# Routed experts by sorted blocks in place of dense expert units

## Chip, cores and metric

The kernel runs on 1 core of one Trainium2 chip. The metric is the device time of one execution in microseconds, the median of several runs.

## What is computed

Two transformer layers over x of 2 x 512 tokens with 256 features: a grouped-query attention with ternary weights, a gated MLP of width 1024 with a Walsh-Hadamard transform, a time-mixing recurrence (scan over the tokens) and a mixture of experts. Each part is normalised, goes through its layer, is normalised again and added to x. The change lies in the last part, here cut to its core:

```python
logits = x @ gate_w                      # E = 32 experts
probs = jax.nn.softmax(logits, axis=-1)
topw, topi = jax.lax.top_k(probs, K)     # K = 4
topw = topw / jnp.sum(topw, axis=-1, keepdims=True)
combine = jnp.zeros((T, E), x.dtype).at[jnp.arange(T)[:, None], topi].set(topw)
def body(acc, ew):
    wg_e, wu_e, wd_e, c_e = ew           # F = 96 features per expert
    h = jax.nn.silu(x @ wg_e) * (x @ wu_e)
    return (acc + c_e[:, None] * (h @ wd_e), None)
out, _ = jax.lax.scan(body, jnp.zeros_like(x), (wg, wu, wd, combine.T))
shared = jax.nn.silu(x @ sg) * (x @ su) @ sd     # SF = 704 features
out = out + jax.nn.sigmoid(x @ seg) * shared
```

## The kernel before

The program is written by hand, one instruction stream an engine, with semaphores between them (`wait_ge`, `then_inc`). Tokens are kept as 8 tiles of 128 rows (`xa`, `xb`); a batch b is four of them, T = 512 tokens. For products the rows are transposed to columns and split into two fp32r parts, high and low (`cols_hi`, `cols_lo`), and each product is three passes (hi x hi, lo x hi, hi x lo; `three_passes`, L1472 to L1474).

The features of all experts and of the shared expert are laid in one row of E*F + SF = 3776 and cut into MC = 30 chunks of 128. Every chunk is computed for every token of a batch, so there are 60 expert units v. Of a unit, SP loads the chunk's weights (`load_chunk`, 384 KB, into one of four places), ACT casts them to the high part (`chunk_high`, L1298), POOL subtracts for the low part (`chunk_low`, L638). PE makes gate and linear product (`expert_up`: twelve matmuls of 512 columns), ACT takes the silu (L1240), DVE multiplies (`expert_unit`, L1095), and PE's select matmul (L1680) spreads each token's weight of the expert over the chunk's features:

```python
pe.matmul(ps[:, (3 * r + 2) % 4, :], select_sb[:, bass.ds(chunk * P, P)],
          ct[:, cs], start=True, stop=True).then_inc(bc_full, 1)
```

A token that didn't choose the expert has weight 0 there. DVE multiplies by it (L1100), ACT and DVE split the result (L1246, L1104), and PE adds it to the output (`expert_down`, twelve matmuls of 256 columns, L1484) in PSUM; the down product of unit v - 1 stands behind the up product of unit v.

The order of the work is written out. The 30 units of batch 0 are interleaved by hand with the time mixing of batch 1 (`keys`, `values`, `receptances` after units 2, 3 and 6, the output product after 14, batch 1's transposes and logits after 18 to 20; on DVE `mixes`, `read_keys`, `scan`, `out_stats`, `out_apply`, `in_apply`), so batch 1's mixing is spread over 20 units. Two units on, batch 1's 30 follow, most of them in a loop of four units. Routing (`route_top`, `route_weights`, `route_split`, L1012 to L1076) finds the four largest logits of each token. After the last unit DVE takes statistics of the output in PSUM (`out_stats`), POOL raises the variance to -1/2 (`power`, L518), DVE and ACT scale, add and shift (`out_apply`, `shift`) and SP stores.

## Time and profile before

| | us |
|---|---|
| runs shown: median (lowest to highest) | 691.62 (690.61 to 692.38) |
| span of the profiled execution, from its first to its last instruction | 690.5 |
| PE busy in it | 581.9 |
| DVE busy | 451.5 |
| ACT busy | 311.6 |
| POOL busy | 251.7 |
| batch 0's first unit starts | 370.7 |
| last matmul starts | 681.3 |

The profile's page gives no other time of that execution; its span stands within the runs shown. Busy times overlap: a matmul's record reaches from its start to its last write, and the next one starts before that, so the distance between two starts is what a matmul costs in a stream. Durations are of one execution, on the one core.

### The profile page before, as it was taken

To read this page: it belongs to the slowest core of one execution; us is meant where nothing else is said; L and a number is where in the kernel's file an instruction comes from. 1 tells how busy PE (TensorE), PEld (TensorE's weight loads), DVE (VectorE), ACT (ScalarE), POOL (GpSimd) and SP (SyncE) were. 2 spreads that over 40 slices of the span, in tenths; PEclk is the share of its full clock that TensorE was granted. 3 is DMA by queue.
4 is the path that set the end of the run, shared out by engine and by line. 5 is a ranking of instruction groups with operands and counts; after the bars stand their busy time and mean duration, and the time that the engine had idled before them with its cause. 6 is when DMAs were issued, how large, how long until landed. Compare 5 with 4: busy or idle time off the path is not lost.

```text
span 690.5 us, 11130 instructions
## 1 busy us (share of the span) xinstructions
PE 581.9 (84%) x3618; PEld 420.6 (61%) x3618; DVE 451.5 (65%) x881; ACT 311.6 (45%) x511; POOL 251.7 (36%) x294
## 2 busy tenths in 40 slices
PE   0358999999998897988626879998989989999994
PEld 0244544554443486766524667886768868888883
DVE  5898767877773667555888658758675464444444
ACT  1132556666676532275115563433534444444442
POOL 5821233343447314031030632443324434444440
PEclk9976599999999999999768989999999999999998
DMA  6063210111330013000020112231222222222310
GB/s 171 0 162 97 59 38 22 34 35 36 112 111 1 12 47 58 0 1 1 0 91 0 47 47 68 84 101 46 69 69 78 89 82 80 88 89 90 91 54 30
DMA packets 25627, 41.22 MB, mean 60 GB/s; under 512 B 3640, under 2 KB 17272, under 8 KB 25592
## 3 DMA queue, kind: packets, MB, share of 16 engines
q1 hardware_dynamic: 25160, 39.72, 19.5%
q0 software_dynamic: 432, 1.05, 0.9%
q8 instruction: 20, 0.33, 0.2%
q14 instruction: 15, 0.12, 0.1%
HBM read 37.81 MB, written 3.80 MB: 60 GB/s over the span
## 4 chain that ended last, share of the span: by engine, by line
PE 57%; DVE 25%; issue 7%; ACT 6%; POOL 3%; DMA 1%; SPq 1%; POOLq 0%; DVEq 0%; ACTq 0%
PE ps L1484 9%; PE ps L1472 7%; PE ps L1473 7%; PE ps L1474 7%; PE ps L1424 7%; PE ps L1553 6%; PE ps L1435 6%; PE ps L1427 2%; DVE st L756 2%; DVE xn L684 2%; ACT h_hi L1246 2%; DVE hf L1100 2%; DVE sg L1095 2%; PE ps L1680 1%; DVE negm L844 1%
## 5 line engine op out<-in xcount | busy, mean ns | idle before, releaser
L638 POOL TENSOR_TENSOR mslot_lo<-mraw,mslot_hi 128x768 fp32r<-128x768 f32 x60 | 112.2, 1870 | 176.7 <-ACT mslot_hi L1298 176.7
L844 DVE TENSOR_REDUCE negm<-ps 128x1 f32<-128x512 f32 (+2 forms) x192 | 107.6, 593 | 36.7 <-PE ps L1427 35.6
L1246 ACT CAST h_hi<-hf 128x512 fp32r<-128x512 f32 x76 | 47.2, 621 | 181.3 <-DVE hf L1100 144.1
L1208 ACT ACTIVATE probs<-ps 128x512 f32<-128x512 f32 x160 | 91.9, 597 | 66.7 <-PE ps L1435 66.0
L1472 PE MATMUL ps<-cols_hi,mslot_hi 128*128 128x512 f32 x240 | 96.4, 402 | 3.7 <-ACT sg L1240 2.2
L1473 PE MATMUL ps<-cols_hi,mslot_lo 128*128 128x512 f32 x240 | 94.3, 393 | 0.0
L1474 PE MATMUL ps<-cols_lo,mslot_hi 128*128 128x512 f32 x240 | 93.7, 390 | 0.0
L1095 DVE TENSOR_TENSOR sg<-sg,ps 128x512 f32<-128x512 f32 x60 | 41.0, 683 | 75.0 <-PE ps L1474 58.3
L1484 PE MATMUL ps<-mslot_hi,h_hi 128*128 128x256 f32 x240 | 78.0, 325 | 9.0 <-DVE h_lo L1104 9.0
L1424 PE MATMUL ps<-k_all,q_all 72*128 (+4 forms) x256 | 73.8, 330 | 9.2 <-DMA q_all<-q_parts_scratch 7.4
L1104 DVE TENSOR_TENSOR h_lo<-hf,h_hi 128x512 fp32r<-128x512 f32 x60 | 41.5, 692 | 41.2 <-ACT h_hi L1246 41.2
L1435 PE MATMUL ps<-q_all,k_all 75*128 (+4 forms) x256 | 65.9, 321 | 3.1 <-ACT probs L1208 2.3
L1484 PE MATMUL ps<-mslot_hi,h_lo 128*128 128x256 f32 x240 | 67.7, 282 | 0.0
L1484 PE MATMUL ps<-mslot_lo,h_hi 128*128 128x256 f32 x240 | 67.7, 282 | 0.0
L518 POOL TENSOR_TENSOR rstd<-ve,halfneg 128x4 f32<-128x4 f32 x16 | 16.2, 1011 | 119.3 <-DVE ve L787 72.7
L1240 ACT ACTIVATE sg<-ps 128x512 f32<-128x512 f32 x76 | 45.2, 595 | 27.2 <-PE ps L1474 26.0
L1424 PEld LDWEIGHTS ps<-k_all,q_all 72*128 72x128 bf16 (+1 forms) x256 | 25.9, 104 | 49.9 <-issue 30.1
L1427 PE MATMUL ps<-hide_cols,identb 128*128 128x128 bf16 x256 | 54.7, 234 | 0.0
L1472 PEld LDWEIGHTS ps<-cols_hi,mslot_hi 128*128 128x128 f32 x240 | 45.7, 190 | 14.3 <-ACT sg L1240 3.1
L1484 PEld LDWEIGHTS ps<-mslot_hi,h_hi 128*128 128x128 f32 x240 | 46.1, 192 | 11.5 <-DVE h_lo L1104 11.4
L1474 PEld LDWEIGHTS ps<-cols_lo,mslot_hi 128*128 128x128 f32 x240 | 45.2, 188 | 10.1
L1298 ACT CAST mslot_hi<-mraw 128x768 fp32r<-128x768 f32 x60 | 49.8, 831 | 2.3 <-PE ps L1484 2.3
(221 smaller groups left out, 1176.7 us busy)
## 6 DMA issues: line engine op xcount, KB each, us to landing
mraw<-in_moe_w SPq DMA_DIRECT2D x60, 384.0 KB, 3.1
q_all<-q_parts_scratch SPq DMA_DIRECT2D x48, 96.0 KB
q_parts_scratch<-qparts SPq DMA_DIRECT2D x6, 256.0 KB, 2.5
k_parts_scratch<-kparts SPq DMA_DIRECT2D x6, 192.0 KB, 3.8
k_all<-k_parts_scratch SPq DMA_DIRECT2D x6, 192.0 KB
xa<-in_x SPq DMA_DIRECT2D x2, 512.0 KB, 4.9
w2a<-in_w SPq DMA_DIRECT2D x1, 1024.0 KB, 8.0
w1raw<-in_w SPq DMA_DIRECT2D x2, 512.0 KB, 5.4
```

Of the source, the lines that this page charges most:

```text
L638: pool.tensor_tensor(mslot_lo[:, place, :], mraw[:, place, :], mslot_hi[:, place, :].bitcast(F32), ALU.subtract)\
L844: dve.tensor_reduce(negm[:, par, qt, h0:h0 + nh], ps[:, u % 4, 0:nh * w].rearrange("p (h t) -> p h t", h=nh), AX.X, ALU.max, negate=True). ...
L1095: dve.tensor_tensor(sg[:, par, :], sg[:, par, :], ps[:, (3 * r + 1) % 4, :], ALU.mult).then_inc(t_done, 1)
L1208: act.activation(probs[:, par, u, :], ps[:, 4 + u % 2, :], ACT.Exp)\
L1246: act.copy(h_hi[:, par, :], hf[:, par, :]).then_inc(h_hi_done, 1)
L1424: pe.matmul(ps[:, u % 4, c:c + w], q_all[0:72, bass.ds(g * (GQ * T) + (h * T + qt * P), P)], k_all[0:72, bass.ds(g * T, w)], start=True, s ...
L1427: mm = pe.matmul(ps[:, u % 4, c + w - P:c + w], identb[:, :], hide_cols[:, :], start=False, stop=True)
L1435: mm = pe.matmul(ps[:, 4 + u % 2, c:c + w], k_all[0:75, bass.ds(g * T + kt * P, P)], q_all[0:75, bass.ds(g * (GQ * T) + (h * T + kt * P), w)],
L1472: pe.matmul(out, lhs_hi, rhs_hi, start=first, stop=False)
L1473: pe.matmul(out, lhs_lo, rhs_hi, start=False, stop=False)
L1474: return pe.matmul(out, lhs_hi, rhs_lo, start=False, stop=last)
L1484: mm = pe.matmul(z_tile(part, b, t), h[:, par, ts], w, start=start and n == 0 and t % 2 == 0, stop=False, skip_group_check=True)
```

## The change

The routed experts are computed only for tokens that chose them. All of this is new: for each (token, choice) the row gets a place in a DRAM table `x_sorted` of 63 blocks of 128 rows, each block of one expert. 63 = 4096 / 128 + 31 bounds what any routing can need. PE counts, with triangular and all-one matrices, how many tokens ahead chose the same expert (`ranks`); DVE turns ranks into destinations and the blocks' experts into a table (`route_places`, `block_experts`), batch 0 first, so that batch 0's rows can go before batch 1's routing is known. ACT copies each row four times with its number n*4 + j behind it (`rows_with_ids`, 260 floats), and POOL scatters tile by tile with indirect DMAs (`scatter`, 32 in all). The table is filled with padding rows first, by seven DMAs of SP, whose number is out of bounds.

The shared expert keeps the old way, in six chunks of its own (`shared_up`, `shared_down`, 12 units u = 16 + s for both batches), without select matmul; ACT multiplies the result with the token's sigmoid gate (`shared_rows`). Batch 1's mixing now stands between the six units of batch 0; ranks and the table's row stand between those of batch 1. The weights of all experts are loaded once into SBUF (`wgu` 6.3 MB, `wd` 3.1 MB, fp32).

Then come 63 blocks. SP loads a block's rows, PE transposes them, reads the block's expert from `etab` into a register, multiplies with its gate and up weights (fp32, 2 x 96 columns), transposes the gated result and multiplies with its down weights; DVE copies the transposes out and gates, ACT does silu and the output copy, POOL scatters the 128 output rows to `y_slots` by their numbers, out-of-bound ones skipped. At the end SP loads `y_slots`, four rows a token, and DVE adds them with the token's weights (`combine`, L1348 of the changed file).

```diff
+FIRST_SHARED = E * F // P
+SHARED = MC - FIRST_SHARED
+BLOCKS = N * TOPK // P + E - 1
+XW = D + 4
+XR, YR, CR = 4, 4, 4
...
+            sp.wait_ge(s_pad, 2)
+            for n in range(7):
+                sp.dma_start(
+                    x_sorted[n * 9 * P:(n + 1) * 9 * P, :].rearrange("(b p) f -> p b f", p=P),
+                    pad[:, :].unsqueeze(1).to_broadcast((P, 9, XW))).then_inc(s_sorted, 16)
...
+            sp.wait_ge(proj_r, DC * B)
+            load_up(1)
+            sp.wait_ge(z_done, 2 * B)
+            load_up(0)
+
+            for r in range(2):
+                sp.wait_ge(scattered[r], 16 * TOPK * TILES // 2)
+            for i in range(BLOCKS):
+                if i >= XR:
+                    sp.wait_ge(bt_done, i - XR + 1)
+                    sp.wait_ge(bt_copied, i - XR + 1)
+                sp.dma_start(xblk[:, i % XR, :], x_sorted[i * P:(i + 1) * P, :])\
+                    .then_inc(xb_in[i % XR], 16)
+            for r in range(YR):
+                sp.wait_ge(y_out[r], 16 * len(range(r, BLOCKS, YR)))
+            for t in range(TILES):
+                if t >= CR:
+                    sp.wait_ge(yc_read, t - CR + 1)
+                sp.dma_start(
+                    ycomb[:, t % CR, :, :].rearrange("p j d -> p (j d)"),
+                    y_slots.rearrange("(t p j) d -> t p (j d)", p=P, j=TOPK)[t])\
+                    .then_inc(yc_in[t % CR], 16)
             for b in range(B):
...
+            def scatter(u):
+
+                pool.wait_ge(dest_ready, u // TPB + 1)
+                pool.wait_ge(xr_ready, 2 * u + 2)
+                for j in range(TOPK):
+                    pool.indirect_dma_start(
+                        out=x_sorted, out_offset=bass.IndirectOffsetOnAxis(
+                            ap=dest[:, u, j:j + 1], axis=0),
+                        in_=xr[:, u % 2, j, :], in_offset=None).then_inc(scattered[u % 2], 16)
...
+            for i in range(BLOCKS):
+                pool.wait_ge(by_ready, i + 1)
+                pool.indirect_dma_start(
+                    out=y_slots, out_offset=bass.IndirectOffsetOnAxis(
+                        ap=ids[:, i:i + 1], axis=0),
+                    in_=yblk[:, i % YR, :], in_offset=None, bounds_check=N * TOPK - 1,
+                    oob_is_err=False).then_inc(y_out[i % YR], 16)
...
+            def block_in(i):
+
+                dve.wait_ge(bt_done, i + 1)
+                if i >= 2:
+                    dve.wait_ge(bu_done, i - 1)
+                dve.tensor_copy(xcol[:, i % 2, :], ps[:, i % 2, 0:D])
+                dve.tensor_copy(ids[:, i:i + 1], xblk[:, i % XR, D:D + 1]).then_inc(bt_copied, 1)
...
+            def block_gate(i):
+
+                dve.wait_ge(b_silu, i + 1)
+                if i >= 2:
+                    dve.wait_ge(bh_done, i - 1)
+                dve.tensor_tensor(hb[:, i % 2, :], gb[:, i % 2, :], ps[:, 2 + i % 2, F:2 * F],
+                                  ALU.mult).then_inc(b_mul, 1)
...
+            def block_hidden(i):
+
+                dve.wait_ge(bh_done, i + 1)
+                if i >= 2:
+                    dve.wait_ge(bd_done, i - 1)
+                dve.tensor_copy(hcol[0:F, i % 2, :], ps[0:F, 6 + i % 2, 0:P])\
+                    .then_inc(bh_copied, 1)
...
+                            ins = dve.scalar_tensor_tensor(
+                                xa[:, t, :], ycomb[:, t % CR, j, :], wtop[:, t, j:j + 1],
+                                xa[:, t, :], ALU.mult, ALU.add)
...
+            def rows_with_ids(u):
+
+                act.wait_ge(rows_ready, (NORMS.index((2, u // TPB)) + 1) * TPB)
+                act.wait_ge(s_ids, 1)
+                if u < 2:
+                    act.wait_ge(m_lo_ready, SHARED)
+                else:
+                    act.wait_ge(scattered[u % 2], 16 * TOPK * (u // 2))
+                act.copy(xr[:, u % 2, :, 0:D],
+                         rows[:, u, :].unsqueeze(1).to_broadcast((P, TOPK, D))).then_inc(xr_ready, 1)
+                act.copy(xr[:, u % 2, :, D:XW],
+                         idf[:, u, :].unsqueeze(2).to_broadcast((P, TOPK, XW - D)))\
+                    .then_inc(xr_ready, 1)
...
+            def block_silu(i):
+
+                act.wait_ge(bu_done, i + 1)
+                if i >= 2:
+                    act.wait_ge(b_mul, i - 1)
+                act.activation(gb[:, i % 2, :], ps[:, 2 + i % 2, 0:F], ACT.Silu)\
+                    .then_inc(b_silu, 1)
...
+            def block_out(i):
+
+                act.wait_ge(bd_done, i + 1)
+                if i >= YR:
+                    act.wait_ge(y_out[i % YR], 16 * (i // YR))
+                act.copy(yblk[:, i % YR, :], ps[:, 4 + i % 2, 0:D]).then_inc(by_ready, 1)
...
+            def block_in(i):
+
+                pe.wait_ge(xb_in[i % XR], 16 * (i // XR + 1))
+                if i >= 2:
+                    pe.wait_ge(bt_copied, i - 1)
+                else:
+                    pe.wait_ge(silu_done, B * (HC + SHARED))
+                    pe.wait_ge(mul_done, B * (HC + SHARED))
+                for k in range(DC):
+                    mm = pe.transpose(ps[:, i % 2, k * P:(k + 1) * P],
+                                      xblk[:, i % XR, k * P:(k + 1) * P], ident[:, :])
...
+            def block_up(i, e):
+
+                pe.wait_ge(bt_copied, i + 1)
+                if i >= 2:
+                    pe.wait_ge(b_mul, i - 1)
+                for k in range(DC):
+                    mm = pe.matmul(
+                        ps[:, 2 + i % 2, 0:2 * F].rearrange("p (w f) -> p w f", w=2),
+                        xcol[:, i % 2, k * P:(k + 1) * P], wgu[:, k, :, bass.ds(e * F, F)],
+                        start=k == 0, stop=k == DC - 1)
+                mm.then_inc(bu_done, 1)
...
+            def block_hidden(i):
+
+                pe.wait_ge(b_mul, i + 1)
+                if i >= 2:
+                    pe.wait_ge(bh_copied, i - 1)
+                pe.transpose(ps[0:F, 6 + i % 2, 0:P], hb[:, i % 2, :], ident[:, :])\
+                    .then_inc(bh_done, 1)
...
+            def block_down(i, e):
+
+                pe.wait_ge(bh_copied, i + 1)
+                if i >= 2:
+                    pe.wait_ge(by_ready, i - 1)
+                pe.matmul(ps[:, 4 + i % 2, 0:D], hcol[0:F, i % 2, :],
+                          wd[0:F, bass.ds(e, 1), :].rearrange("p o d -> p (o d)"),
+                          start=True, stop=True).then_inc(bd_done, 1)
...
-            expert_up(0, 0, 0, 0)
-            for v in range(1, MC):
-                expert_up(v, v % 4, 0, v)
-                expert_down(v - 1, (v - 1) % 4, 0, start=v == 1)
...
-            with pe.Fori(0, (MC - 2) // 4) as i:
-                for r in range(4):
-                    q = (MC + 2 + r) % 4
-                    expert_up(i * 4 + (MC + 2 + r), q, 1, i * 4 + (2 + r))
-                    expert_down(i * 4 + (MC + 1 + r), (q + 3) % 4, 1)
-            expert_down(2 * MC - 1, (2 * MC - 1) % 4, 1)
...
+            shared_up(6)
+            ranks(1)
+            shared_up(7)
+            shared_down(6)
+            block_row()
+            for s in range(8, 2 * SHARED):
+                shared_up(s)
+                shared_down(s - 1)
+            shared_down(2 * SHARED - 1)
...
+            experts = {}
+            for i in range(BLOCKS + 3):
+                if i < BLOCKS:
+                    block_in(i)
+                if 0 <= i - 1 < BLOCKS:
+                    experts[i - 1] = pe.value_load(etab[0:1, i - 1:i], min_val=0, max_val=E - 1)
+                    block_up(i - 1, experts[i - 1])
+                if 0 <= i - 2 < BLOCKS:
+                    block_hidden(i - 2)
+                if 0 <= i - 3 < BLOCKS:
+                    block_down(i - 3, experts.pop(i - 3))
 
...```

Three places where the order of instructions moves: PE's loop over experts against its blocks, PE's shared units, and POOL. First PE, in the loop over batch 1's expert units before: the end of an up product, the select matmul, the start of a down product. `L1680 ISA` computes the address of the chunk's select columns.

```order
L1474 MATMUL ps<-cols_lo,mslot_hi 128x512
L1472 MATMUL ps<-cols_hi,mslot_hi 128x512
L1473 MATMUL ps<-cols_hi,mslot_lo 128x512
L1474 MATMUL ps<-cols_lo,mslot_hi 128x512
L1680 ISA [waits hidden_product_done]
L1680 MATMUL ps<-ct,select_sb 128x512
L1484 MATMUL ps<-mslot_hi,h_hi 128x256 [waits hidden_lo_ready]
L1484 MATMUL ps<-mslot_hi,h_lo 128x256
L1484 MATMUL ps<-mslot_lo,h_hi 128x256
```

These matmuls, the select matmul with them, are gone for every unit that was a routed expert's; twelve shared units keep the rest. PE now, one turn of the block stage (transposes of block i, load of block i - 1's expert and its up product, hidden transpose of i - 2, down product of i - 3). `ident` is the unit matrix, `etab` the table of the blocks' experts, `block_rows_out` ACT's output copy.

```order
L1977 MATMUL ps<-ident,xblk 128x128 [waits block_columns_copied,block_rows_loaded_1]
L1977 MATMUL ps<-ident,xblk 128x128
L2081 TENSOR_LOAD etab
L2081 ISA x2
L1987 ISA [waits block_gated,block_columns_copied]
L1987 MATMUL ps<-wgu,xcol 128x192
L1987 ISA
L1987 MATMUL ps<-wgu,xcol 128x192
L1998 MATMUL ps<-ident,hb 96x128 [waits block_hidden_copied,block_gated]
L2006 ISA [waits block_rows_out,block_hidden_copied]
L2006 MATMUL ps<-wd,hcol 128x256
```

A loop of long passes in one format has become 63 written-out turns of short fp32 products, with a register load and five other register steps in each.

PE now, between shared units 6 and 8 (`schunks` are the split weights of shared chunks, `blkB` holds each block's expert, one a partition):

```order
L1752 MATMUL ps<-schunk_164,h_lo 128x256
L1752 MATMUL ps<-schunk_164,h_hi 128x256
L1965 MATMUL ps<-ident,blkB 1x128 [waits block_experts_ready]
L1740 MATMUL ps<-cols_hi,schunks 128x512 [waits silu_done]
L1741 MATMUL ps<-cols_hi,schunks 128x512
L1742 MATMUL ps<-cols_lo,schunks 128x512
L1740 MATMUL ps<-cols_hi,schunks 128x512
```

The matmul of L1965, which waits for DVE's whole computation of places and experts, stands ahead of the up product of shared unit 8 and all that follow.

POOL now, its last scatters into the sorted table, the block stage's scatters and the two powers of the end (`rows_with_ids_ready` is ACT's copy of the rows, `block_rows_out` that of a block's output); before, this place held a `TENSOR_TENSOR mslot_lo` for each unit:

```order
L754 DMA x_sorted_scratch<-xr,dest 8064x260 x3
L754 DMA x_sorted_scratch<-xr,dest 8064x260 [waits rows_with_ids_ready,destinations_ready]
L754 DMA x_sorted_scratch<-xr,dest 8064x260 x3
L785 DMA y_slots_scratch<-yblk,ids 4096x256 [waits block_rows_out] x63
L621 TENSOR_TENSOR rstd<-ve,halfneg 128x4 [waits ln_variance_ready] x2
```

POOL's work for the weights is gone from here, and each block's output now passes through one of its 63 indirect DMAs.

## Rows read from the trace of the kernel before

**Rows 1.** The page, part 1: busy us (share of the span) xinstructions.
```profile
PE 581.9 (84%) x3618; PEld 420.6 (61%) x3618; DVE 451.5 (65%) x881; ACT 311.6 (45%) x511; POOL 251.7 (36%) x294
```

**Rows 2.** Windows: length, busy us of PE, PEld, DVE, ACT, POOL, clock, DMA share, GB/s.
```profile
500.00:600.00 100.00, 93.58 (x523) 76.85 (x522) 54.51 (x100) 43.11 (x69) 37.97 (x22) 1.00 0.27 80
```

**Rows 3.** Line 1680, 520 to 680 us: min/median/max ns, starts; idle before it.
```profile
L1680 PE MATMUL ps<-ct,select_sb x35: 389/390/390, 523.5 to 676.8; 128*128 128x512 bf16 x35
L1680 PEldq FUSED_REGOPS  x28: 55/55/65, 551.0 to 673.4; - x28
...
  issue: 9.2, 35
```

**Rows 4.** Timeline of PE, 540 to 560 us: start us, us, engine, line.
```profile
540.03 0.39 PE L1473 MATMUL ps<-cols_hi,mslot_lo 128*128 128x512 f32 x1
540.26 0.39 PE L1474 MATMUL ps<-cols_lo,mslot_hi 128*128 128x512 f32 x1
```

**Rows 5.** Groups by line and form: busy us, mean ns | idle before.
```profile
L638 POOL TENSOR_TENSOR mslot_lo<-mraw,mslot_hi 128x768 fp32r<-128x768 f32 x60 | 112.2, 1870 | 176.7 <-ACT mslot_hi L1298 176.7
...
L1095 DVE TENSOR_TENSOR sg<-sg,ps 128x512 f32<-128x512 f32 x60 | 41.0, 683 | 75.0 <-PE ps L1474 58.3 <-ACT sg L1240 16.5
```

**Rows 6.** Timeline of DVE: the two copies of the routing logits.
```profile
368.96 0.29 DVE L1012 COPY logits<-ps 128x136 f32<-128x136 f32 x1
...
498.14 0.29 DVE L1012 COPY logits<-ps 128x136 f32<-128x136 f32 x1
```

**Rows 7.** Groups by form: mixed columns, the second scan, the reciprocals.
```profile
L948 DVE RECIPROCAL gain<-den 128x256 f32<-128x256 f32 x8 | 13.8, 1740 | 0.0
...
L916 DVE SCALAR_TENSOR_TENSOR mixed<-xT,vec,mix 128x512 f32<-128x512 f32 x12 | 11.7, 1014 | 3.0 <-ACT mix L1262 3.0
...
L943 DVE TENSOR_TENSOR_SCAN num<-decay,num 128x512 f32<-128x512 f32 x4 | 4.8, 1196 | 0.0
```

**Rows 8.** Timeline of DVE: first and last of the normalisation of batch 1's rows.
```profile
468.56 1.28 DVE L773 TENSOR_TENSOR rows<-ps,bo_sb 128x512 f32<-128x512 f32 x2
...
482.69 2.93 DVE L824 TENSOR_SCALAR rows<-xb,rstd,nmr 128x256 f32<-128x256 f32 x4
```

**Rows 9.** Timeline of PE in attention, 100 to 112 us.
```profile
100.80 0.22 PE L1427 MATMUL ps<-hide_cols,identb 128*128 128x128 bf16 x1
100.86 0.22 PE L1424 MATMUL ps<-k_all,q_all 72*128 x1
...
102.66 0.60 PE L1523 MATMUL ps<-ident,o_cols 128*128 128x128 f32 x4
...
106.84 1.06 PE L1553 MATMUL ps<-probs,v_now 128*32 128x512 f32 x8
```

**Rows 10.** DMA issues: queue, KB, median us from issue to landing.
```profile
out_x<-xa SPq DMA_DIRECT2D x2, 512.0 KB, 3.6
...
iota<-in_consts SPq DMA_DIRECT2D x1, 16.0 KB, 1.8
```

**Rows 11.** Timeline of SP's queue, start of the kernel.
```profile
1.35 0.48 SPq L388 DMA_DIRECT2D ident<-in_consts  x1
```

**Rows 12.** Timeline of POOL, start of the kernel: a plain DMA of 128 rows.
```profile
1.53 0.73 POOL L510 DMA_DIRECT2D identb<-in_consts  x1 [0.31 <-POOL halfneg L508]
```

**Rows 13.** Windows of 4 us, columns as in rows 2.
```profile
48.00:52.00 4.00, 0.85 (x3) 0.40 (x4) 3.97 (x2) 0.00 (x0) 3.21 (x1) 0.50 0.98 224
...
72.00:76.00 4.00, 4.00 (x22) 2.42 (x20) 2.74 (x6) 2.39 (x4) 0.79 (x2) 0.50 0.31 59
...
384.00:388.00 4.00, 2.25 (x10) 1.50 (x11) 2.07 (x3) 2.52 (x5) 2.69 (x3) 1.00 0.19 73
...
400.00:404.00 4.00, 3.20 (x8) 2.52 (x9) 0.75 (x2) 3.97 (x6) 1.14 (x1) 0.50 0.00 0
```

**Rows 14.** Timeline of all engines, 681 to 691 us.
```profile
683.77 1.01 POOL L518 TENSOR_TENSOR rstd<-ve,halfneg 128x4 f32<-128x4 f32 x1 [10.70 <-DVE ve L787]
...
684.89 1.65 DVE L807 SCALAR_TENSOR_TENSOR xa<-ps,rstd,xb 128x256 f32<-128x256 f32 x4
```

667 lines of the change are left out of this document (418 added, 249 removed).

## Prediction

> **What bounds the kernel now.** I read the page first (busy shares), then windows over the routed stage, then the groups of instructions, then the timelines of the places that the change rebuilds. PE is busy 84% of the 690.5 us span [rows 1], and in the routed stage 93.58 us of the 100 between 500 and 600 us at the full granted clock [rows 2]. From 523.5 to 676.8 us the select matmul, of which each expert unit has one, starts 35 times [rows 3]: (676.8 - 523.5) / 34 = **4.51 us a unit**. Its 512-column matmuls stand 0.23 us apart [rows 4]; the pause of 0.26 us before each select matmul ends with "issue" (9.2 us over 35) [rows 3]. Without select and pause the unit is 4.51 - 0.23 - 0.26 = 4.02 us. DVE's three operations of 0.69 us and POOL's 1.87 us a unit lie beside it [rows 5]. So a removed unit is worth 4.51 us of the end, as long as nothing else then sets the pace.
>
> **What goes.** 60 units become 12 (six shared chunks, once per batch): 48 x 4.51 = **216.5 us**. Their loads, casts and subtractions lay under PE and are worth nothing more. What hung behind them comes to light, and three new parts are added.
>
> **1. Batch 1's mixing loses its cover.** Routing of batch 0 starts at 368.96 us [rows 6]; before it nothing changes but the seven stores of padding rows (8.4 MB), which SP issues behind attention and nobody waits for before batch 0's scatters. From there DVE must do, in order: routing, weights and places of batch 0 (9.5 us, counted like part 2), six mixed columns at 1.01 (7.4 with gaps), decay and gain reads (3.1), two scans of 1.20 for each half with a product before them, 6.3, four reciprocals of 1.74 [rows 7], six products and remainders of 0.7 (4.3), the normalisation of batch 1's rows, six shared units of two operations (8.3) and the column split (1.3). The normalisation ran from 468.56 to 485.6 us before [rows 8], with two expert units between its parts; alone I make it 11.5. Together 58.7 us of DVE. What DVE waits for in this chain (ACT's multiply and cast at each mix, three projections of 12 matmuls at 0.23, the output product, the cast inside each unit, the transposes and the logits at the end) adds some 29. Batch 1's logits then stand at 369 + 88 = 457 us; before they came at 498.14 [rows 6], because 20 units stood between.
>
> **2. Places and experts for batch 1.** Routing top with the mask 4.5 us, then some 24 short DVE operations with a settle between most, 0.2 us each, an array product of 0.69 and its reduction: 10.5 us, to 472. PE stands still for about 5 of it, since the matmul that turns the expert table into a row is ahead of shared unit 8 in PE's order. Then four units (16.1), the last down (1.4), the last unit's four hops of up to 0.69 on ACT and DVE [rows 5] (2.6) and the four scaled copies (2.0): 494, and **497 us** when the first block's rows are in. Sixteen scatters run beside this on POOL, four to a tile, two tile buffers. At 1.3 us each (below) they end at about 493, just covered; at 2.5 they cost 15 to 20 us.
>
> **3. 63 blocks.** Per block and warm, PE streams three fp32 transposes (0.11 us each: four in 0.60 us with one latency [rows 9]), two fp32 products of 192 columns and one of 256. Eight fp32 records of 512 columns, four column groups side by side, take 1.06 us [rows 9]; less the latency that is 0.43 us a record, twice 512 columns, and there are two records to a product: four column times each, 0.64 + 0.43 us. Sum 0.33 + 1.07 = **1.40 us**. In the middle stands the register load of the block's expert. Below: a register operation on PE takes 0.055 us [rows 3]. Above: a 16 KB load lands in 1.8 us [rows 10]. I take 0.8, above SP's DMA issue of 0.48 [rows 11] and nearer to it than to the load, as it is one small read by a sequencer. PE's sequencer then needs nine load-matmul pairs at 0.06 (two starts at 100.80 and 100.86 [rows 9]), five register steps (0.3) and the load, 1.6 us. It doesn't run wholly beside the stream: two waits at 0.26, as before the select matmul [rows 3], and some 0.3 of the load stay open. 1.40 + 0.52 + 0.3 = **2.2 us a block**. The floor is 1.6 (the sequencer alone); the ceiling 2.8 (stream at half clock) or 3.05 (POOL, below).
> The Trainium skill (DMA: Bandwidth & Descriptors, section on latency and other measured facts) gives such a register load a floor of about 600 ns; by it the block would be 2.0 us and the end 664. No row here shows it.
> Beside PE: DVE's four copies are about 1.1 us, ACT's two 0.6, SP's issue 0.48. The DMA engines move up to 264 KB a block; at the 224 GB/s that 1 KB rows reached at 48 us with a share of 0.98 [rows 13] that is 1.2 us. None sets the pace. POOL's indirect issue is shown nowhere. Below: a plain issue for 128 rows, 0.73 us [rows 12]. Above: that plus a read of its list at 1.8 us, 2.5, or 3.05 if its wait for ACT's copy isn't overlapped. I take 1.3, nearer the plain one, as the list is 512 bytes and the descriptors are as many; it hides under 2.2. 63 x 2.2 = **138.6 us**, plus 4 to fill.
>
> **4. The tail.** Before, from the last matmul to the end, 9.5 us. Now: the last scatter (4.5), the first load of 512 KB of slots (3.6, as the output store [rows 10]), for each batch sixteen multiply-adds at 0.42, statistics 2.1, POOL's power 1.01 with two hops 1.3, four more multiply-adds 1.65 [rows 14], so 2 x 12.2, and the last shift and store (4). Together **36.6 us**, 27.1 more.
>
> **Sum.** 497 + 4 + 138.6 + 36.6 = **676.2 us** of span. By differences: 690.5 - 216.5 + 142.6 + 27.1, and 32.5 of batch 1's chain that had lain under experts. The profiled span is 690.5, the median of the runs 691.6, so I add 1: **677 us**. The expert weights' load (9.4 MB) starts at about 415 and 440 us; at half the rate of [rows 13] its second half is in by 470, so I cost it at nothing. Its cover is the 25 us to 495.
>
> **Rivals.**
> - *The blocks starve TensorE (slower).* PE streams 1.40 us in 2.2. The granted clock from 72 to 76 us is 0.50 although PE counts as busy throughout, and from 400 to 404 it is 0.50 (1.2 GHz) after a pause [rows 13]. At 1.2 GHz the stream alone is 2.8 us: 497 + 4 + 176.4 + 36.6 = 714. It decides from 2.43 us a block on. Against it: 384 to 388 us has 2.25 us of 4 busy and stays at 1.00 [rows 13]. The Trainium skill (TensorE: Matmul & The Clock Gate, Part 1) says that the throttled state is the default and activity releases it; by that rule a stage with a pause in every block may stay throttled. The trace has both outcomes. 15%.
> - *POOL's indirect issue is the pace (slower).* At 2.5 us, 63 x 2.6 = 164, and batch 1's sixteen scatters end some 15 us after the shared units: 716. For it: 63 of them in one chain, and the simplest 4-element operation costs POOL 1.01 us [rows 14]. Against: the plain issue. 22%.
> - *The handshakes vanish (faster).* Stream and sequencer overlap wholly, 63 x 1.7 = 107: 645. 13%.
> - *The threshold.* A block of 2.42 us: 690, no difference. 5%.
> - *It doesn't do what it says.* All 63 blocks run, full or not; were the 3968 padding rows stored instead of skipped, only DMA time under PE would grow. No chance of its own.
>
> **How the numbers follow.** The forecast (1.9 to 2.38 us a block) has 0.40, the fast case 0.13: faster 0.53. Threshold 0.05. Clock 0.15, POOL 0.22, and 0.05 for a chain of batch 1 or a tail longer by over 15 us: slower 0.42. Under 0.3%, 2 us, this measurement can't tell a difference from none. The low end, 638, is 1.6 us a block; the high end, 745, the POOL case with 3.05 us. The forecast's own range is 658 to 688.
>
> **What would show it.** PE's blocks should repeat every 2.2 us from about 497 us on, at a granted clock over 0.9, with the idle time before the 192-column product put to issue. DVE's second logits copy should stand near 457 us, the last matmul near 640. If the 63 indirect issues stand end to end on POOL and ACT's copy into yblk waits for a scatter, POOL is the pace; if the clock reads 0.5 over the blocks, it is the clock. Blocks of over 2.43 us, a start after 510 or a tail over 50 would make the prediction wrong.

## The result, and the profile after

The changed kernel took **654.66 us** (median of four runs, 652.24 to 659.02) against 691.48 before, a ratio of 0.9471 with a 95% interval of 0.9436 to 0.9507. The forecast was 677 us, 14.6 us faster than the 691.6 shown; the change brought 36.8. The range of 638 to 745 holds the time, the size of the gain is off by a factor of 2.5. The profiled execution is the longest of the four: 659.02 us, span 657.1.

The same kernel was measured four times more, each time on a different chip and beside the kernel before on that chip. It took 641.35, 657.67, 641.44 and 655.42 us, the kernel before 691.0 to 691.7 each time. So there are two levels, medians of 641 and of 655 to 658 (single runs 652 to 662), and the first measurement is on the upper one; what is known of the difference is taken up below. As each level came with its chips, a property of the chip can't be told from one of the occasion.

The page of the changed kernel, parts 1 (busy), 2 (forty slices of 16.4 us) and 5 (groups), which answer to [rows 1]:

```profile
PE 479.6 (73%) x2991; PEld 335.5 (51%) x2991; DVE 411.7 (63%) x1017; ACT 264.9 (40%) x511; POOL 246.0 (37%) x341
...
PE   0367999999998898879863617753695999999500
...
PEclk9986689999999999798976757985997899999855
...
L785 POOL DMA_INDIRECT y_slots_scratch<-yblk,ids x63 | 62.0, 984 | 62.6 <-ACT yblk L1633 38.8
...
L754 POOL DMA_INDIRECT x_sorted_scratch<-xr,dest x32 | 31.8, 992 | 50.8 <-DVE dest L1246 26.1
```

The window over the blocks is the one at the right, nine tenths busy at full clock; the dip before it is batch 1's chain, where the clock reads 0.5 to 0.9. An indirect DMA holds POOL for 0.98 us.

Windows of the changed kernel (length, busy us of PE, PEld, DVE, ACT, POOL, clock, DMA share, GB/s), two over the chain, one over the blocks, one over the tail:

```profile
369.00:400.00 31.00, 13.87 (x59) 11.21 (x59) 17.00 (x31) 19.75 (x32) 14.45 (x9) 0.65 0.54 107
...
430.00:460.00 30.00, 14.03 (x70) 12.72 (x71) 14.69 (x40) 7.67 (x15) 9.75 (x10) 0.70 0.59 188
...
540.00:560.00 20.00, 19.22 (x108) 15.56 (x108) 10.81 (x49) 7.00 (x24) 11.82 (x13) 1.00 0.43 125
...
620.00:640.00 20.00, 0.00 (x0) 0.00 (x0) 12.11 (x34) 1.70 (x4) 1.79 (x2) 0.50 0.58 210
```

One undisturbed turn of the block stage on PE, from its timeline (start, length, engine, operation, records). The next turn's transposes (L1977) start 1.52 us after these:

```profile
549.91 0.39 PE L1977 MATMUL ps<-ident,xblk 128*128 128x128 f32 x2
550.14 0.91 PE L1987 MATMUL ps<-wgu,xcol 128*128 x4
550.89 0.27 PE L1998 MATMUL ps<-ident,hb 128*96 128x128 f32 x1
551.00 0.60 PE L2006 MATMUL ps<-wd,hcol 96*128 x2
551.44 0.38 PE L1977 MATMUL ps<-ident,xblk 128*128 128x128 f32 x2
```

PE's sequencer (PEldq) at L2081, the register load of a block's expert, and the operations it brings with it (min/median/max ns, first and last start):

```profile
L2081 PEldq TENSOR_LOAD <-etab x63: 296/300/481, 508.4 to 613.6; - x63
L2081 PEldq FUSED_REGOPS  x63: 151/151/165, 509.0 to 613.9; - x63
L2081 PEldq SEQ_ASSERT  x63: 18/18/28, 509.2 to 614.2; - x63
```

Against the forecast's landmarks: batch 1's routing starts 97.9 us after batch 0's (88 forecast, 457 us; here 463.4 after 365.5). The first block's columns are copied at 508.7 us (497 for its rows). The last matmul ends at 617.5 us, so the blocks take 108.8 us (142.6 with the fill), 33.8 less. The tail takes 39.6 us (36.6). 676.2 + 11.7 - 33.8 + 3.0 = 657.1, the span. (Columns come 0.7 us after the start of the block's transposes.)

### The profile page after: what moved, and what is told of

The parts are those of the page before. It is cut to its first block, busy times and chain, and to the rows that moved or that the text cites. A ratio compares the mean times of both kernels' runs of the same rounds, so it can differ in the third digit from the quotient of the medians.

```text
span 657.1 us, 10360 instructions
## 1 busy us (share of the span) xinstructions
PE 479.6 (73%) x2991; PEld 335.5 (51%) x2991; DVE 411.7 (63%) x1017; ACT 264.9 (40%) x511; POOL 246.0 (37%) x341
## 2 busy tenths in 40 slices
PE   0367999999998898879863617753695999999500
## 4 chain that ended last, share of the span: by engine, by line
PE 50%; DVE 26%; issue 10%; ACT 6%; POOL 2%; DMA 2%; another core or an unknown queue 1%; SPq 1%; POOLq 0%; DVEq 0%; ACTq 0%
PE ps L1987 7%; PE ps L1692 7%; PE ps L1821 6%; PE ps L1703 6%; PE ps L1752 4%; PE ps L2006 4%; DVE st L880 2%; PE ps L1740 2%; PE ps L1695 2%; DVE xn L808 2%; PE ps L1977 2%; PE ps L1741 2%; DVE gain L1073 2%; PE ps L1742 2%; DVE hf L1025 2%
## 5 line engine op out<-in xcount | busy, mean ns | idle before, releaser
L1427 ACT ACTIVATE probs<-ps 128x512 f32<-128x512 f32 x160 | 91.8, 597 | 63.6 <-PE ps L1703 62.9
L785 POOL DMA_INDIRECT y_slots_scratch<-yblk,ids x63 | 62.0, 984 | 62.6 <-ACT yblk L1633 38.8
L1987 PE MATMUL ps<-wgu,xcol 128*128 x252 | 58.1, 354 | 1.8 <-DVE ids L1312 0.5
L621 POOL TENSOR_TENSOR rstd<-ve,halfneg 128x4 f32<-128x4 f32 x16 | 16.3, 1016 | 100.3 <-DVE ve L911 53.1
L1692 PEld LDWEIGHTS ps<-k_all,q_all 72*128 72x128 bf16 (+1 forms) x256 | 25.6, 103 | 51.7 <-issue 31.8
L754 POOL DMA_INDIRECT x_sorted_scratch<-xr,dest x32 | 31.8, 992 | 50.8 <-DVE dest L1246 26.1
L1465 ACT CAST h_hi<-hf 128x512 fp32r<-128x512 f32 x28 | 17.3, 619 | 81.2 <-DVE hf L1025 74.5
L1821 PE MATMUL ps<-probs,v_now 128*32 128x128 f32 (+3 forms) x512 | 47.9, 450 | 0.7 <-DVE att L994 0.7
L1987 PEld LDWEIGHTS ps<-wgu,xcol 128*128 128x128 f32 x252 | 40.3, 193 | 9.2 <-issue 6.1
L1025 DVE TENSOR_TENSOR hf<-sg,ps 128x512 f32<-128x512 f32 x28 | 19.1, 683 | 41.2 <-ACT sg L1459 18.1
L1319 DVE TENSOR_TENSOR hb<-gb,ps 128x96 f32<-128x96 f32 x63 | 15.9, 253 | 40.6 <-ACT gb L1625 21.1
L665 POOL TENSOR_SCALAR_AFFINE_SELECT probs<-probs 128x512 f32<-128x512 f32 x64 | 39.8, 634 | 0.0
L2006 PE MATMUL ps<-wd,hcol 96*128 x126 | 38.6, 389 | 1.2 <-DVE hcol L1327 1.2
L1752 PE MATMUL ps<-schunks,h_hi 128*128 128x256 f32 x80 | 21.1, 346 | 23.1 <-DVE h_lo L1030 23.1
L1311 DVE COPY xcol<-ps 128x256 f32<-128x256 f32 x63 | 26.5, 422 | 14.2 <-PE ps L1977 12.6
L1625 ACT ACTIVATE gb<-ps 128x96 f32<-128x96 f32 x63 | 15.9, 252 | 48.3 <-PE ps L1987 43.4
L1633 ACT COPY yblk<-ps 128x256 f32<-128x256 f32 x63 | 23.4, 372 | 23.6 <-PE ps L2006 15.6
## 6 DMA issues: line engine op xcount, KB each, us to landing
ycomb<-y_slots_scratch SPq DMA_DIRECT2D x8, 512.0 KB, 4.4
```

The source lines that it names most:

```text
L665: pool.affine_select(out=tiles, in_=tiles, compare_op=ALU.is_ge, fill=0.0, base=0, pattern=[[0, GQ], [1, P]], channel_multiplier=-1).then_ ...
L785: pool.indirect_dma_start(out=y_slots, out_offset=bass.IndirectOffsetOnAxis(ap=ids[:, i:i + 1], axis=0), in_=yblk[:, i % YR, :], in_offset ...
L1025: dve.tensor_tensor(hf[:, par, :], sg[:, par, :], ps[:, bank + 1, :], ALU.mult)\
L1427: act.activation(probs[:, par, u, :], ps[:, 4 + u % 2, :], ACT.Exp)\
L1692: pe.matmul(ps[:, u % 4, c:c + w], q_all[0:72, bass.ds(g * (GQ * T) + (h * T + qt * P), P)], k_all[0:72, bass.ds(g * T, w)], start=True, s ...
L1752: mm = pe.matmul(z_tile(part, b, t), h[:, par, ts], w, start=start and n == 0 and t % 2 == 0, stop=False, skip_group_check=True)
```

## The experiments

Block periods are read from DVE's gating (`tensor_tensor(hb, ...)`, once in a block): last start less first start, by 62. These rows, from the view of tile hb, carry most verdicts; where a kernel's steady period is 1.4 to 1.5 us, a single one of over 1.9 is called a lapse. In order: the changed kernel, then c0, e1, e2, e5, e8, c3 and e13 as they come below.

```profile
L1319 DVE TENSOR_TENSOR hb<-gb,ps x63: 242/253/255, 510.6 to 615.7; 128x96 f32<-128x96 f32 x63
```
```profile
L1319 DVE TENSOR_TENSOR hb<-gb,ps x63: 253/254/255, 504.3 to 599.1; 128x96 f32<-128x96 f32 x63
```
```profile
L1319 DVE TENSOR_TENSOR hb<-gb,ps x63: 253/255/255, 505.5 to 593.8; 128x96 f32<-128x96 f32 x63
```
```profile
L1319 DVE TENSOR_TENSOR hb<-gb,ps x63: 253/253/255, 504.8 to 631.9; 128x96 f32<-128x96 f32 x63
```
```profile
L1319 DVE TENSOR_TENSOR hb<-gb,ps x63: 253/253/255, 504.0 to 591.1; 128x96 f32<-128x96 f32 x63
```
```profile
L1319 DVE TENSOR_TENSOR hb<-gb,ps x63: 253/255/255, 507.6 to 642.3; 128x96 f32<-128x96 f32 x63
```
```profile
L1319 DVE TENSOR_TENSOR hb<-gb,ps x63: 240/254/255, 512.1 to 616.4; 128x96 f32<-128x96 f32 x63
```
```profile
L1316 DVE TENSOR_TENSOR hb<-gb,ps x63: 253/254/255, 514.8 to 609.1; 128x96 f32<-128x96 f32 x63
```

That is 1.70 us for the changed kernel, 1.53 for c0 (the same kernel), 1.42, 2.05, 1.40, 2.17, 1.68 and 1.52 us.

### What a block costs: fixed experts, up product twice

The two edits:

```diff
-                    experts[i - 1] = pe.value_load(etab[0:1, i - 1:i], min_val=0, max_val=E - 1)
+                    experts[i - 1] = (i - 1) % E
...
-                        xcol[:, i % 2, k * P:(k + 1) * P], wgu[:, k, :, bass.ds(e * F, F)],
+                        xcol[:, i % 2, k * P:(k + 1) * P], wgu[:, k, :, e * F:(e + 1) * F],
```

> Each block takes a fixed expert (its number modulo 32) whose weights are addressed by constants, so the register load and the address steps are gone; the result is that of other experts than the routed ones. Theory A, TensorE's stream of 1.5 us is the pace and the sequencer works ahead of it: the block period stays at 1.69 us on the mean (within 0.05), the time at 654 +- 4 us. Rival B, the step of the forecast, the load lies partly in the open, now in the 0.19 us by which the mean period is over 1.50: the period falls to about 1.5 us and the time by 10 to 12 us. Rival C, the sequencer itself is the pace: the period falls by the 0.6 us that its load and address steps last, the time by over 30 us.

(The down product's weights are addressed by constants in the same way; that line isn't shown.) Measured: 632.19 us over two runs, 627.29 and 637.08. The profile is of the longer; why the shorter is 9.8 us less isn't known, the changed kernel wasn't run beside them, and nothing below rests on this time. From the third period on, all are 1.42 us, but for a shorter last one. In [rows 9] the forecast had read 1.40 us of stream; 1.42 is what TensorE takes when nothing else sets the pace. None of the three theories gave this price: A's unchanged 1.69 is out, B's 1.5 and C's fall of 0.6 are both off. Against a kernel without lapses (1.53, below) the fall is 0.1 us: the sequencer was the pace, as C has it, but the stream stands right under it and catches the gain.

```diff
-                for k in range(DC):
+                for k in [*range(DC), *range(DC)]:
```

> The up product of each block is computed twice into the same accumulator (the second time from the start again), which adds four matmul records and nothing for any other engine. Theory A, TensorE's stream is the pace: the four records take 0.91 us from first start to last end and about 0.65 us of the stream, so the block period goes from 1.69 to 2.3 us and the time from 654 to about 694. Rival B, the period is made of handshakes with slack in the stream: it grows by under 0.4 us, the time by under 25 us.

Measured: 675.22 us, 59 of 62 periods at 2.07. That is 2.07 - 1.42 = 0.65 us for four more records, on top of the stream without the load, as theory A has it, and not on top of the period with it (1.53 + 0.65 = 2.18). With a longer stream the register load costs nothing that these periods show. So the two run beside each other, and what is longer counts. Theory A was right on this and wrong on which of the two is longer in the kernel as it is: e1 shows that the sequencer is, by 0.1 us.

### Plain output, half the blocks

```diff
-                pool.indirect_dma_start(
-                    out=y_slots, out_offset=bass.IndirectOffsetOnAxis(
-                        ap=ids[:, i:i + 1], axis=0),
-                    in_=yblk[:, i % YR, :], in_offset=None, bounds_check=N * TOPK - 1,
-                    oob_is_err=False).then_inc(y_out[i % YR], 16)
+                pool.dma_start(y_slots[i * P:(i + 1) * P, :], yblk[:, i % YR, :])\
+                    .then_inc(y_out[i % YR], 16)
```

> Each block's output is written by a plain DMA of POOL to 128 rows in a row instead of being scattered by token, so that the sums at the end take rows of other tokens, and all 63 blocks store their 128 rows where the scatter left out the padding. Theory A, TensorE's stream is the pace and POOL is beside it: period 1.69 us, time 654 +- 4. Rival D, the indirect DMAs cause the lapses (a block of 2.3 to 2.5 us every four to five): the period falls to 1.50 to 1.55 us, the time by 9 to 12 us.

> As the kernel with plain output DMAs, but only 32 of the 63 blocks are run, so that half of the routed sums is left out. With that kernel it gives the price of a block and of all that is not a block. Theory A: 31 blocks less at 1.69 us, 52 us less (600 to 603 us); if the lapses go with the indirect DMAs, 31 x 1.52 = 47 us less. By the forecast's price of 2.2 us it would be 68 us less. Start and tail: first block's columns at 508 us and 40 us from the last matmul to the end, as in the changed kernel.

(With both, `y_slots` has room for all 63 blocks' rows; e4 is e3 with each engine's loop over the blocks cut to 32.) Measured: 641.09 and 591.11 us. 50.0 us for 31 blocks, 1.61 each; 31 periods of 1.53 are 47.4 of it, the rest is mostly in the tail (37.9 us against 35.3 from the last matmul on). The forecast's 2.2 us would have made 68. At the time I took the missing lapses for the effect of the plain DMA, as Rival D has it. That conclusion needed the changed kernel beside it, and the next measurement had that.

### The changed kernel again, three waits less

> The changed kernel as it is, beside the others of this call. All theories: 652 to 657 us, a block's median period 1.57 us and its mean 1.66 to 1.70, some 15 lapses of over 1.9 us among 62 periods; first block's columns copied between 502 and 509 us.

Measured: 641.35 us (641.30 to 642.25), ratio 0.9287 (0.9257 to 0.9317), no period over 1.9 us, columns at 501.7. My expectation was wrong: the lapses aren't there in every measurement of this kernel.

```diff
             def block_in(i):
...
-                if i >= 2:
-                    pe.wait_ge(bt_copied, i - 1)
-                else:
+                if i < 2:
...
             def block_up(i, e):
...
-                if i >= 2:
-                    pe.wait_ge(b_mul, i - 1)
...
             def block_hidden(i):
...
-                if i >= 2:
-                    pe.wait_ge(bh_copied, i - 1)
```

> Three of TensorE's waits in a block that an earlier wait of its own already implies (transposes on the copy of two blocks back, up product on the gating two back, hidden transpose on the hidden copy two back) are taken out; the computation is the same. Theory S, the sequencer is the pace (1.52 us a block, of which the waits are 3 x 0.05) and the stream (1.42 us) is just below it: the sequencer now needs 1.37, the stream sets the pace, the period becomes 1.42 us throughout as with fixed experts and the lapses go; time 15 to 18 us less, 637 to 640. Rival L, the lapses have a cause of their own in the register load beside the indirect DMAs: the median falls to 1.42 but lapses of 0.8 us stay at every fourth to fifth block, time only 8 us less. Rival A, the stream is the pace already: no change.

Measured: 634.32 us, 7.0 below the control; nearly every period 1.42. 62 x (1.529 - 1.405) = 7.7. The median is as theory S has it: taking work from the sequencer alone, with no change to any product, brings the block to the stream's 1.42 us. (The price of 0.05 us for a wait stays an assumption: the stream stopped the fall, so the run shows the three to be worth at least 0.1.) The 15 us it forecast counted on lapses, of which this control has none. e1 and e5 give the stream the same 1.42 with two different sequencer programs. So in the changed kernel **the sequencer sets the period at 1.52, with TensorE's stream 0.1 under it**. Where the lapses sit is seen in the waits of e1 and c0 (without) and of the changed kernel's first measurement (with), each over 540 to 590 us (waiter, releaser: us, times, longest):

```profile
ACT gb L1625 <- PE ps L1987: 18.0, 36, 0.5
DVE hb L1319 <- ACT gb L1625: 16.1, 36, 0.5
```
```profile
ACT gb L1625 <- PE ps L1987: 20.1, 33, 0.7
```
```profile
ACT gb L1625 <- PE ps L1987: 19.1, 22, 2.0
...
POOL y_slots_scratch L785 <- ACT yblk L1633: 9.2, 6, 2.0
```

Without lapses ACT's longest wait for an up product is 0.5 and 0.7 us; with them it is 2.0.

### The register load doubled

```diff
+                    pe.value_load(etab[0:1, i - 1:i], min_val=0, max_val=E - 1)
                     experts[i - 1] = pe.value_load(etab[0:1, i - 1:i], min_val=0, max_val=E - 1)
```

> Each block's expert is loaded into a register of TensorE twice, the first time unused; the computation is the same. Theory S, the sequencer is the pace and a register load takes 0.30 us for itself and 0.17 us for the two operations behind it: the period rises from 1.53 to 2.0 us, the time by 29 us to 670. The forecast's price of 0.8 us for a load: the period rises to 2.3, the time by 50. Rival A, the stream is the pace and sequencer work is hidden: under 10 us more.

Measured: 685.63 us; the period is 2.17 against c0's 1.53 without lapses, **0.64 us for a register load** with its two operations, of which 0.47 are the records at L2081 and 0.17 gaps between them. Theory S's mechanism holds, its price was low by the gaps (685.63 us for its 670); the forecast's 0.8 us was high by 0.16. The changed kernel beside it (c1, below) had lapses; here the longest period is 2.31, and ACT's silu starts within 0.04 us of the up product's recorded end in every block. The Trainium skill (DMA: Bandwidth & Descriptors, section on latency and other measured facts) gives such a load a floor of about 600 ns; the record itself is 0.30 us here, and the whole step on the sequencer 0.64.

### POOL twice as long

```diff
+                pool.indirect_dma_start(
+                    out=y_twice, out_offset=bass.IndirectOffsetOnAxis(
+                        ap=ids[:, i:i + 1], axis=0),
+                    in_=yblk[:, i % YR, :], in_offset=None, bounds_check=N * TOPK - 1,
+                    oob_is_err=False).then_inc(y_out[i % YR], 16)
```

> Each block's output is scattered twice, the second time to a table that nobody reads, so that POOL has two indirect DMAs of 0.98 us with a gap of 0.30 us each in a block. All theories: POOL becomes the pace at 2.58 us a block, 63 x 2.58 = 163 against 106 us, time 654 + 56 = 710 us. Clock: the forecast's rival says that TensorE, streaming 1.42 of 2.58 us, falls to half clock; then its records stretch (up product from 0.91 to over 1.3 us) and the stream of 2.8 us sets a period of 2.85 us or more, time 727. Against it, the clock stays at 1.00 and the period at 2.58.

(The second table `y_twice` and the doubled counts in the waits for the scatters aren't shown.) Measured: 708.52 us (ratio 1.0255, 1.0212 to 1.0299), mean period 2.43. Two windows of this kernel over the blocks, and POOL's timeline in it:

```profile
520.00:560.00 40.00, 32.62 (x146) 21.21 (x144) 13.50 (x64) 8.31 (x32) 30.55 (x32) 1.00 0.42 127
560.00:600.00 40.00, 30.84 (x134) 19.54 (x133) 12.60 (x61) 8.41 (x32) 30.55 (x32) 1.00 0.39 117
```
```profile
560.88 0.98 POOL L791 DMA_INDIRECT y_twice_scratch<-yblk,ids  x1 [0.30 <-issue]
562.17 0.98 POOL L786 DMA_INDIRECT y_slots_scratch<-yblk,ids  x1 [0.30 <-issue]
```

POOL's records, one every 1.29 us, fill the 40 us, and TensorE, waiting in every block, keeps full clock. (It reads 0.91 from 600 to 640 us.) So pauses of 2.43 - 1.42 = 1.0 us in a block, on the mean, don't bring the clock down to half for the stage. (The mean lies under the 2.58 of two issues because the first eight blocks pass at 1.4 to 1.8 before POOL's queue is full.) The forecast's rival on POOL was right in its mechanism and wrong in its price: an indirect issue repeats every 1.29 us, which the forecast had at 1.3, and at 1.29 it hides under 1.52.

### Batch 1's chain

In the changed kernel's timeline two waits stand out (at the row's end: idle time before, releaser). PE, at shared unit 0's down product, which waits for DVE's places of batch 0 and has batch 1's key projection behind it:

```profile
391.87 0.58 PE L1752 MATMUL ps<-schunk,h_hi 128*128 128x256 f32 x1 [17.13 <-DVE dest L1246]
392.25 0.41 PE L1752 MATMUL ps<-schunk,h_lo 128*128 128x256 f32 x1
...
394.59 0.63 PE L1740 MATMUL ps<-m_hi,rwhi 128*128 128x512 f32 x1
395.02 0.63 PE L1741 MATMUL ps<-m_hi,rwlo 128*128 128x512 f32 x1
```

After the pause of 17.1 us the records of 512 columns stand 0.43 us apart, twice the 0.23 of [rows 4]: the clock is at its lower level, 1.2 GHz. And POOL, whose power for batch 1's normalisation stands behind batch 0's sixteen scatters, with DVE's input and what waited for it:

```profile
442.35 0.96 POOL L754 DMA_INDIRECT x_sorted_scratch<-xr,dest  x1 [0.30 <-issue]
443.33 1.06 POOL L621 TENSOR_TENSOR rstd<-ve,halfneg 128x4 f32<-128x4 f32 x1
```
```profile
439.84 0.19 DVE L911 TENSOR_SCALAR ve<-mv 128x4 f32<-128x4 f32 x1
444.42 0.16 DVE L927 SCALAR_TENSOR_TENSOR nmrz<-mv,rstd 128x4 f32<-128x4 f32 x1 [4.39 <-issue]
```

The two edits that take both out of the way:

```diff
             shared_up(1)
-            shared_down(0)
             keys(1)
+            shared_down(0)
...
-            for u in range(TPB):
+            for u in range(TPB - 1):
                 scatter(u)
             power(12)
             power(13)
+            scatter(TPB - 1)
```

> Batch 1's key projection goes ahead of shared unit 0's down product on TensorE, so that it no longer waits for DVE's places of batch 0, and POOL's two powers for batch 1 go ahead of the last four of batch 0's sixteen scatters. Theory Q, these two queues hold up batch 1's chain (TensorE stood 17.1 us before that down product and its 2.9 us at half clock, the power came 3.3 us after its input): the second logits copy comes 6 to 9 us earlier, at 455 to 457 instead of 463.4, and the time falls by as much. Rival, DVE's own work is the chain there and fills the gap: under 2 us.

Measured: 633.13 us, 8.2 below the changed kernel beside it (641.35), within theory Q's 6 to 9. The second logits copy comes 85.9 us after the first instead of 96.3, a little more than theory Q gave, and the first block's columns at 493.3 instead of 501.7. It beats both kernels, with a ratio of 0.9166 (0.9136 to 0.9195) to the kernel before. What each of the two edits is worth wasn't measured.

```diff
-                for w in range(2):
+                warm = [0, 0]
+                for w in [0, 1] if s != 1 else [0, 0, 0, 0, 1, 1, 1, 1]:
...
-                    mm.then_inc(up_u if w else up_g, 1)
+                    warm[w] += 1
+                    if s != 1 or warm[w] == 4:
+                        mm.then_inc(up_u if w else up_g, 1)
```

> Shared unit 1's up product is computed four times over instead of once, 8.3 us more of TensorE's work, put where it stands idle for 17.1 us in batch 1's chain; same result, no other engine has more to do. Theory K, part of the 7 us by which the chain was longer than forecast is half clock after such pauses: with TensorE busy up to DVE's places, the down product of unit 0 and the first half of the key projection behind it run at full clock, 0.12 and 0.23 us apart instead of 0.21 and 0.43, and the second logits copy comes 2 to 3.5 us earlier, and the time falls as much. Rival, the clock does not rise or the chain is DVE's: 0 +- 1 us.

Measured: 661.68 us (658.86 to 664.16) against a control of 657.67; the logits come 97.3 us after the first, 0.6 earlier than in the control. In its timeline of PE:

```profile
394.06 0.58 PE L1752 MATMUL ps<-schunk,h_hi 128*128 128x256 f32 x1 [9.50 <-DVE dest L1246]
394.44 0.41 PE L1752 MATMUL ps<-schunk,h_lo 128*128 128x256 f32 x1
394.65 0.63 PE L1752 MATMUL ps<-schunk,h_hi 128*128 128x256 f32 x2
...
398.06 0.53 PE L1740 MATMUL ps<-m_hi,rwhi 128*128 128x512 f32 x1
398.43 0.39 PE L1741 MATMUL ps<-m_hi,rwlo 128*128 128x512 f32 x1
```

A miss: the repeated product covers only half of the pause, TensorE stands another 9.5 us, and the down product behind it still runs at half clock (0.21 us apart for 256 columns); the key projection is back at full clock from its fifth matmul on. How much of the chain's length the clock makes was not isolated. The first columns come 7 us after the control's (511.4 against 504.3) although the logits don't; the late signals described below stand in between.

### Together, and the lapses

> The changed kernel as it is, once more beside the others. If the lapses of the first measurement are no part of the kernel, this is 640 to 643 us with a block period of 1.53 us; if they are, 652 to 657 us.

This is the control for e8, e9 and e10. Measured: 657.67 us (656.99 to 662.42): the lapses are back, 17 periods over 1.9 us, mean 1.74.

> The three waits less, keys and powers first, and in addition the matmul that turns the expert table into a row behind the last shared unit's down product (with DVE's copy of it), so that no shared unit stands behind DVE's places. The first two are worth 7.0 and 8.2 us and lie in different stages, so they add: 641.3 - 15.2 = 626. The third: the forecast had 5 us for TensorE's standstill there, but in the changed kernel run again the rows of the first block, issued at 498.8 behind POOL's last scatter, come 1.7 us after the shared rows are done, so POOL's sixteen scatters at 1.27 us are the longer branch and it brings nothing: 625 to 628 us. If the shared units were the longer branch: 621 to 623.

The new one of its three edits:

```diff
             shared_down(6)
-            block_row()
...
             shared_down(2 * SHARED - 1)
+            block_row()
...
-                dve.wait_ge(blk_row, 1)
-                dve.tensor_copy(etab[:, :], ps[0:1, 7, 0:64]).then_inc(etab_ready, 1)
...
                 shared_unit(s)
+            dve.wait_ge(blk_row, 1)
+            dve.tensor_copy(etab[:, :], ps[0:1, 7, 0:64]).then_inc(etab_ready, 1)
```

Measured: 650.71 us, 7.0 below the control instead of 15. The first columns come at 496.4 against 504.3, so the chain's part is there. The blocks gain nothing: their shortest steady period is 1.42, but lapses of up to 3.9 us bring the mean to 1.74, the control's. Whether the row matmul's place matters this doesn't tell.

So far no kernel with plain output or without the register load had stood beside a control with lapses. Two more groups of runs were made for that.

> The changed kernel as it is, the control of this call. Where it shows lapses (a dozen or more block periods of over 2.2 us, 655 us), the other two runs tell what they are tied to; where it shows none, 641 us, they repeat what is known.

> Plain output DMAs in place of the indirect ones, as before; the sums at the end take rows of other tokens. Beside a control with lapses: Rival D, they come with indirect DMAs in flight: no period over 2.2 us in the block stage, mean 1.53 us, and the time 10 to 13 us under the control. Rival N, they have to do with neither the output nor its kind: a dozen lapses here too, the time within 3 us of the control.

> Fixed experts by constants in place of the register load, indirect output kept; the result is that of other experts than the routed ones. Beside a control with lapses: if they need the register load, every period is 1.42 us; if they come with indirect DMAs alone, lapses stay and the mean is 1.55 to 1.7 us.

Measured: 641.44, 643.21 and 637.66 us. The control has no lapse (mean 1.53), so the three only repeat what was known: without lapses plain output brings nothing (1.54), fixed experts 1.42.

> The changed kernel as it is, the control of this call: 641 us with a block period of 1.53 us, or with lapses 652 to 658 us.

> Plain output DMAs once more. Beside a control with lapses: none in the block stage and 10 to 13 us under the control if they come with indirect DMAs in flight, within 3 us of it if not. Beside a control without: 641 to 643 us.

> The three waits less, keys and powers first, and the row matmul behind the shared units, once more. Beside a control without lapses the first two add: 641.3 - 15.2 = 626 us (625 to 628), and the third brings nothing since POOL's scatters are the longer branch; beside one with lapses 7 us under the control, as in the call before.

Measured: 655.42, 646.26 (641.57 and 650.96) and 646.81 us. This control has lapses, 12 periods over 1.9 us, mean 1.68. The plain output beside it has none, mean 1.52, and its time is 9.2 us under the control (forecast 10 to 13), with its two runs 9.4 apart. POOL's record in it:

```profile
L785 POOL DMA_DIRECT2D y_slots_scratch<-yblk x63: 539/539/597, 518.3 to 611.6; - x63
```

So here the lapses of the block stage come with its indirect DMAs, shown by one profile without them against two with (c3 and e14). Something more is needed, for c0 and c2 have the same DMAs and no lapse, and e8, beside c1, has one such DMA every 2.17 us and no late signal in its blocks. Whether they need the register load too is open: the kernels with fixed experts never stood beside a control with lapses. e14 repeats e9: 8.6 us under its control, mean period 1.69. The sum of the two single edits, 626 us, was met by neither run of them together; both had lapses, and without them it wasn't measured.

What a lapse looks like, in ACT's timeline of the changed kernel: `gb` waits for an up product whose record on PE begins at 531.17 and ends at 532.08, as long as any other, yet ACT is released at 533.02; a turn earlier it was released 0.04 us after the end.

```profile
530.57 0.25 ACT L1625 ACTIVATE gb<-ps 128x96 f32<-128x96 f32 x1 [0.73 <-issue]
531.11 0.37 ACT L1633 COPY yblk<-ps 128x256 f32<-128x256 f32 x1 [0.29 <-issue]
533.02 0.25 ACT L1625 ACTIVATE gb<-ps 128x96 f32<-128x96 f32 x1 [1.54 <-PE ps L1987]
533.80 0.37 ACT L1633 COPY yblk<-ps 128x256 f32<-128x256 f32 x1 [0.53 <-PE ps L2006]
```

The ends of matmuls are modelled, so the profile can't tell whether the product or its signal was late.

The same thing happens ahead of the blocks, and there in e13 too, while batch 1's scatters are in flight. ACT's silu of a shared unit waits for the gate product alone. In e13 the last matmul of such a product starts at 492.77 us, ACT has been free since 495.3, and it is released at 500.72:

```profile
492.77 0.39 PE L1739 MATMUL ps<-cols_lo,schunks 128*128 128x512 f32 x1
```
```profile
500.72 0.60 ACT L1456 ACTIVATE sg<-ps 128x512 f32<-128x512 f32 x1 [5.44 <-remote]
```

e13's first columns come at 512.2 us, against 504.3 for the same kernel without late signals (e11); 2.1 us of that lie ahead of the logits. So the upper level has two parts, late shared units and lapses in the blocks, and the plain output takes away only the second.

One more trait goes with the late signals. The trace notes each change of a semaphore. Between 520 and 600 us it has 1982 and 1969 of them for c0 and c2, and 887 to 910 for the same kernel with lapses (the first measurement, c1, c3). In e13 they are as few before the blocks (111 from 476 to 500 us, 291 in e11) and complete in them (2135, 2120 in e11). No run here was taken without a recording, so whether the recording itself holds the signals up, or both suffer from a third thing, is open.

## Why the prediction was wrong

**The bound and what goes: nothing speaks against it.** With 48 of TensorE's units gone the kernel is 37 us faster in spite of all that came to light; what one unit was worth no run measured.

**Step 3, the block: wrong, and the cause of the miss.** Its inputs were good. Stream 1.40 us (measured 1.42); the sequencer for a turn 1.6 (1.52); POOL's issue 1.3 (1.29); a load 0.8 (0.64). The step that failed is "It doesn't run wholly beside the stream": two waits at 0.26 and 0.3 of the load were added to the stream. e1, e2, e5 and e8 show that nothing is added; the period is the longer of the two. By the forecast's own inputs that is the floor it names, 1.6 us, and 497 + 4 + 63 x 1.6 + 36.6 = 638.4 of span, 639 us: the level of 641. As I read it now (no run tests this), the 0.26 us before the select matmul [rows 3] was a pause in a loop where the waits came one after another with TensorE's work; it was no row for a turn in which the sequencer has its waits behind it while four records of 0.16 us still stream. That the floor's sum lands within 3 us is in part luck: against c0 its start is 4 us early (rows in at 497, transposes at 501.0), its blocks with the fill 5 long (104.8 us, 99.8 measured) and its tail 3 short. In the block the forecast priced a mean of 2.2, and 1.53 without lapses, 1.70 with them, came: 42 and 32 us too much over 63.

**Steps 1 and 2, the start: 4 to 12 us too early.** The chain took 96.3 to 97.9 us for 88. Two queues were missed, both because the added wait was not followed to what stands behind it: batch 0's places, on which shared unit 0's down product and so the keys wait, and the power behind POOL's scatters. e7 shows them together to be worth 10.5 us of the chain and 8.2 us of the time. The half clock in this stage (0.65 and 0.70) was costed nowhere: every duration was taken from warm rows. The chain began 2 to 4 us earlier than in the kernel before, which hid some of it. Then, batch 1's sixteen scatters, 1.26 us apart and more, ended at 497.1 us in c0 and the loads were issued at 498.6, where the forecast had the first rows in at 497. In the first measurement the shared units also lagged, by the late signals described above (columns at 508.7 against 501.7 in c0).

**Step 4, the tail: 3 us short,** 39.6 for 36.6, made of small differences that weren't traced singly. (Its terms for one batch add up to 11.8 us, not to the 12.2 that it used, so by its own terms it is nearer to 4 short.)

**The rivals.** "The handshakes vanish", 1.7 us a block and 645 us at 13%, is what happened, and it should have been the forecast. The clock stayed at 1.00 over the blocks from 514 us on, in e6 from 520 to 600 us too, with far longer pauses (0.91 after that; in c1 and e9 it fell for one short stretch each). In batch 1's chain it did fall, 17 us of pause before it. The Trainium skill's rule (TensorE: Matmul & The Clock Gate, Part 1) that the throttled state is the default and activity releases it agrees with both; what the forecast made of it, that a pause in every block may keep the stage throttled, did not come about. POOL as the pace was a matter of price alone.

**What no step had:** the 13 us between 641 and 655. Nothing in the trace of before could have shown it, and it brought the first measurement nearer to the forecast than the lower level is: that is luck. Against 641 the miss is 36 us.
